# The seam between routing and the expert tiles: ranks ahead of an up product, paddings on two queues, sums ahead of the first weights' low part

## The chip, the cores and the metric

The kernel runs on one core of a Trainium2 chip. A core has five engines, each with a queue of its own that runs in order: TensorE (PE, matmuls), VectorE (DVE), ScalarE (ACT), GpSimd (POOL) and SyncE (SP, which here issues DMAs). They meet at semaphores. The metric is the device time of one execution in microseconds, lower being better.

## What is computed

Two layers over x of shape (4, 1024, 256), each with a cross attention and a feed-forward part, both behind a layer norm and added under a tanh gate:

```python
x = x + jnp.tanh(g_xattn[0]) * _L0_xattn_ref(_layernorm(x), ctx_1024, ctx_1024, mask_BxS2_ik1)
x = x + jnp.tanh(g_ffn[0]) * _L0_ffn_ref(_layernorm(x), ...)     # mixture of experts
x = x + jnp.tanh(g_xattn[1]) * _L1_xattn_ref(_layernorm(x), ctx_1024, ctx_1024, ...)
x = x + jnp.tanh(g_ffn[1]) * _L1_ffn_ref(_layernorm(x), L1_ffn_w_gate, L1_ffn_w_up, L1_ffn_w_down)

def _moe_forward(x, ...):
    logits = (xt @ gate_w.T + gate_b).astype(jnp.float32)
    scores = jax.nn.softmax(logits, axis=-1)
    top_w, top_i = jax.lax.top_k(scores, TOPK)                   # 2 of 8 experts
    ...
    outs = jax.vmap(expert)(w1, b1, w3, b3, w2, b2)              # silu(x w1) * (x w3), then w2
    y = jnp.einsum('etd,te->td', outs, gate_dense)
    z = jax.nn.silu(xt @ ws1.T + bs1) * (xt @ ws3.T + bs3) @ ws2.T + bs2   # shared expert
    return (y + z).reshape(Bq, Sq, D)
```

## The kernel before

The order on every engine is written out by hand; waits on named semaphores tie the engines together. The program has three stages.

**Blocks.** The 4096 tokens are taken in eight blocks (f = 0 to 7) of 512: first attention, second layer norm, the shared expert and the routing. The last block's share of this, f = 7, stands by itself behind the loop, and this is where the change works. On PE, `up(f, m)` for m = 0 to 3 makes a gate half (first bank) and an up half (second bank) of the shared expert's hidden columns, 12 wide matmuls each; `gate_back`, `rank`, `counts`, `pair_limits`, `single_limits` and `tables` are small groups set between them. `down(7, ...)` is the shared expert's second product, with keep-warm matmuls of fixed number before and behind it (24 and 16 rows in the trace).

**Routing.** DVE finds the two best experts of each token (`route_a`), their one-hot form and its sum `routed` (`route_b`), the differences for the softmax (`route_a2`). PE's `rank` counts, by a triangular matrix, the place of each token in its expert's list. DVE's `route_d` and `route_d2` make of it `rrow`, `rank_base` and `pos`. With `pos` POOL scatters the tokens' rows to `rows_by_expert` in DRAM, eight indirect DMAs a block (L677). After the last block PE's `counts` sums up; DVE makes `padpos`, the first free row of each expert, and in three more rounds with PE the tables `tile_expert` and `tile_row`, which tell each expert tile its weights and its rows. SP writes 128 rows of zeros behind each expert's rows ("paddings", 8 DMAs of 128 KB, L475 and L476): for each it reads a register from `padpos` and issues a DMA.

**Expert tiles.** `NU` = 40 tiles, 31 of 256 rows and 9 of 128. `load_weights(u)` and `load_tile(u)` on SP read their place from the tables into a register (L498, L481) and issue the DMA (L502, L494). ACT makes the weights' high part `wph`, DVE the low part `wpl` (`weights_low`, L2384). PE transposes the rows (`tx`, L1322) and runs three matmuls for each product. The first `tx` waits for `shared_done`, which DVE's `shared_out` of the last block gives, and then reads a register.

**Last stage.** Second layer: gathers of the experts' outputs by POOL, attention, feed-forward.

For the shared expert ACT makes the silu of the gate half, DVE's `hidden(f, m)` (L2139) adds the bias and multiplies with the up half, ACT's `hidden_high` makes the high part `hh` and DVE's `hidden_low` (L2053) the low part `hl`. For f = 7, `up(7, 2)` waits for `hidden(7, 0)`, `up(7, 3)` for `hidden(7, 1)`, `down` for `hidden(7, 2)`, and its part k = 3 for `hl` of m = 3.

Of the kernel before, what the change touches and what calls it, by code (L numbers as in the profile page):

```python
# [7 lines left out]
NE, F = 8, 256  # L8
SF, LF = 512, 768
DH, NH = 16, 16  # L10
P = 128
KD = D // P
T = B * S
GT = 4
# [33 lines left out]
def flamingo_kernel(nc, i, out):  # L48
    ctx = ExitStack()
    with ctx:  # L50
        sems = {}

        def sem(name):
            if name not in sems:
                sems[name] = ctx.enter_context(nc.semaphore(name))
            return sems[name]
# [325 lines left out]
        def _(sp):  # L382
# [88 lines left out]
                    small(vo_kept, vo0.rearrange("p b d -> p (b d)"), "l1_out")  # L471

            sp.wait_ge(sem("padpos_done"), 1)
            for e in range(NE):
                row = sp.value_load(padpos[0:1, e:e + 1], min_val=0, max_val=SPARE - P)  # L475
                sp.dma_start(xs[bass.ds(row, P), :], zeros).then_inc(sem("pad_out"), 16)  # L476

# [10 lines left out]

            def load_tile(u):
                src = rows_of_unit(xs, u, 0)  # L490

                if u >= 4:
                    sp.wait_ge(sem("tx_done"), u - 3)
                sp.dma_start(tile_of(xg[u % 4], u), src).then_inc(sem(f"tile_in{u % 4}"), 16)  # L494
# [15 lines left out]
            sp.wait_ge(sem("table_done"), 1)  # L510
            load_weights(0)
            sp.wait_ge(sem("table_done"), 3)
            sp.wait_ge(sem("spare_out"), 16 * 4)
            for p in range(2):
                sp.wait_ge(sem(f"scattered{p}"), NG // 2 * 2 * GT * 16)
            sp.wait_ge(sem("pad_out"), 16 * NE)
            load_tile(0)
            load_tile(1)
            load_weights(1)
# [346 lines left out]
        def _(act):  # L866
# [58 lines left out]
            def silu(f, m):  # L925
                act.wait_ge(sem("u_done"), MS * f + m + 1)

                if above_zero(MS * f + m - 1):
                    act.wait_ge(sem("hl_done"), MS * f + m - 1)
                n = slice(0, now(f) * P)  # L930
                act.activation(sil[m % 2][:, n], up_bank(f, m)[0], ACT.Silu, bias=bs13[:, 0, m:m + 1])\
                    .then_inc(sem("silu_done"), 1)
# [129 lines left out]
            silu(f, 0)  # L1062
            hidden_high(f, 0)
            silu(f, 1)
            hidden_high(f, 1)
            silu(f, 2)
            hidden_high(f, 2)
# [249 lines left out]
        def _(pe):  # L1317
# [390 lines left out]
                last.then_inc(sem("count_mm"), 1)  # L1708

            up(f, 0, lambda: gate_back(f))  # L1710
            up(f, 1, lambda: rank(f))
            counts()
            up(f, 2, pair_limits)
            single_limits()
# [291 lines left out]
        def _(dve):  # L2006
# [163 lines left out]
            def route_b(f):  # L2170

                dve.wait_ge(sem("topi_done"), GT * (f + 1))
                for k in range(2):
                    tt(onehot[:, k, :, :], expert_no.unsqueeze(1).broadcast_to([P, GT, NE]),
                       top8i[:, :, k:k + 1].broadcast_to([P, GT, NE]), ALU.is_equal).then_inc(sem("onehot_done"), 1)
                dve.wait_ge(sem("topi_done"), GT * (f + 1))
                cp(expert_all[:, bass.ds(f, 1), :, :].rearrange("p a k j -> p (a k) j"),
                   top8i[:, :, 0:2].rearrange("p j k -> p k j")).then_inc(sem("route_kept"), 1)
                dve.wait_ge(sem("onehot_done"), 2 * (f + 1))
                tt(routed, onehot[:, 0, :, :], onehot[:, 1, :, :], ALU.add).then_inc(sem("routed_done"), 1)  # L2180

            def route_c(f):

# [147 lines left out]
                step(g, g % 2, nxt=(g + 1 < NG), more=(g + 2 < NG))  # L2331
            f = NG - 1
            route_a(f)
            route_a2(f)
            route_b(f)
            route_d(f)
            route_d2(f, 1, NG // 2 - 1)

# [43 lines left out]
            def weights_low(u):  # L2382
                dve.wait_ge(sem("high_done0"), EARLY[0] + u + 1)
                tt(wpl[u % 2], wraw[u % 3], wph[u % 2], ALU.subtract).then_inc(sem("low_done0"), 1)  # L2384

            hidden(f, 0)
            tile_counts()
            tile_shift()
            hidden_low(f, 0)
# [9 lines left out]
            hidden_low(f, 3)  # L2399
            shift_kept()  # L2400
            route_c(f)
            weights_low(0)
            shared_out(f, 1, (0,))
            shared_out(f, 1, (1,))

            def rows_low(u):
# [431 lines left out]
```

## Time and profile before

| | us |
|---|---|
| timed executions, three | 584.28, 588.28, 591.34 |
| their median | 588.28 |
| the profiled execution | 584.31 |
| span of its instructions | 582.5 |
| PE busy | 561.4 (96%) |
| DVE busy | 452.8 (78%) |
| ACT busy | 376.4 (65%) |
| POOL busy | 258.6 (44%) |

### The profile page before, as it was taken

The page shows a single profiled execution, that of the slowest core. Times are in us where ns is not written, and L with a number is a line of the kernel's source. Part 1 is how long each engine was busy: PE and PEld are TensorE (multiplying, and loading weights), DVE is VectorE, ACT ScalarE, POOL GpSimd, SP SyncE. Part 2 cuts the span into 40 slices and gives each one's busy share as a digit, 9 for nine tenths or more (in the row PEclk, how much of TensorE's full clock was granted, in tenths as well). Part 3 has the DMA queues.
Part 4 walks back from the last instruction along what each step waited for, and adds up shares of the span by engine and source line. Part 5 has one row for each costly group of instructions (what it writes and reads, how often), then busy time and mean ns, then how long its engine had stood idle before and what let it go on. Part 6 is the DMA issues. An engine that isn't in the chain of part 4 may idle for free.

```text
span 582.5 us, 12974 instructions
## 1 busy us (share of the span) xinstructions
PE 561.4 (96%) x3950; PEld 463.8 (80%) x3950; DVE 452.8 (78%) x1248; ACT 376.4 (65%) x729; POOL 258.6 (44%) x291
## 2 busy tenths in 40 slices
PE   8999999999989999999999999989999999999997
PEld 7788888987758999999999998876746656665664
DVE  6989887977636787778887884586999899978765
ACT  5778667776514877768777773255585685785733
POOL 3456557555550134545543444668663740510100
PEclk9999899999979999999999999999999999999999
DMA  8334554352237878888998854762122241100000
GB/s 236 124 121 158 200 191 167 137 186 96 103 134 221 314 238 263 268 271 246 287 279 264 262 191 163 273 231 72 59 64 75 74 151 56 57 17 37 38 37 36
DMA packets 48117, 93.15 MB, mean 160 GB/s; under 512 B 7006, under 2 KB 17322, under 8 KB 47922
## 3 DMA queue, kind: packets, MB, share of 16 engines
q1 hardware_dynamic: 39884, 74.34, 37.8%
q0 software_dynamic: 7440, 17.97, 10.3%
q8 instruction: 33, 0.54, 0.4%
q14 instruction: 34, 0.28, 0.2%
q10 hardware_dynamic: 726, 0.02, 0.1%
HBM read 61.32 MB, written 32.17 MB: 160 GB/s over the span
## 4 chain that ended last, share of the span: by engine, by line
PE 65%; DVE 13%; issue 6%; ACT 5%; POOL 4%; SPq 3%; another core or an unknown queue 2%; DMA 2%; ACTq 0%; DVEq 0%; POOLq 0%
PE bank L1387 13%; PE bank L1389 12%; PE bank L1388 12%; PE bank L1908 10%; PE bank L1322 4%; PE bank L1930 3%; PE bank L1932 3%; POOL yr L775 2%; PE bank L1374 2%; PE bank L1870 2%; POOL rs L789 1%; DVE st L2491 1%; DVE x L2120 1%; SPq L475 1%
## 5 line engine op out<-in xcount | busy, mean ns | idle before, releaser
L727 POOL TENSOR_TENSOR yg<-yg,b 128x512 f32<-128x512 f32 x31 | 46.8, 1510 | 94.4 <-ACT yg L868 94.2
L677 POOL DMA_INDIRECT rows_by_expert<-n,pos x64 | 65.3, 1020 | 36.5 <-DVE pos L2214 20.8
L775 POOL DMA_INDIRECT yr<-expert_out,out_row x64 | 65.2, 1018 | 29.8 <-issue 19.3
L1387 PE MATMUL bank<-xTh,wph 128*128 128x256 f32 x248 | 72.3, 292 | 0.3 <-issue 0.2
L1389 PE MATMUL bank<-xTh,wpl 128*128 128x256 f32 x248 | 70.1, 283 | 0.0
L1388 PE MATMUL bank<-xTl,wph 128*128 128x256 f32 x248 | 70.1, 283 | 0.0
L1908 PE MATMUL bank<-m4Th,wint 128*128 128x512 f16 x192 | 69.0, 380 | 0.9 <-ACT m4Th L868 0.5
L1908 PE MATMUL bank<-m4Tl,wint 128*128 128x512 f16 x192 | 68.9, 379 | 0.4 <-issue 0.4
L2384 DVE TENSOR_TENSOR wpl<-wraw,wph 128x1024 fp32r<-128x1024 f32 x40 | 49.0, 1224 | 11.5 <-ACT wph L868 11.4
L868 ACT ACTIVATE wph<-wraw 128x1024 fp32r<-128x1024 f32 x40 | 42.3, 1058 | 14.3 <-PE bank L1389 9.4
L1387 PEld LDWEIGHTS bank<-xTh,wph 128*128 128x128 f32 x248 | 47.3, 191 | 0.7 <-issue 0.6
L1388 PEld LDWEIGHTS bank<-xTl,wph 128*128 128x128 f32 x248 | 47.4, 191 | 0.0
L1389 PEld LDWEIGHTS bank<-xTh,wpl 128*128 128x128 f32 x248 | 47.4, 191 | 0.0
L1136 ACT ACTIVATE n<-xa,nb,rs 128x256 f32<-128x256 f32 x64 | 34.5, 591 | 14.2 <-DVE nb L2508 13.9
L2564 DVE SCALAR_TENSOR_TENSOR sl<-bank,sl 128x512 f32<-128x512 f32 x48 | 32.7, 687 | 13.7 <-ACT sl L1183 9.9
L1930 PE MATMUL bank<-wint,g3h 128*128 128x256 f16 x192 | 42.6, 273 | 0.6 <-DVE sl L2564 0.5
L1932 PE MATMUL bank<-wint,g3l 128*128 128x256 f16 x192 | 42.5, 272 | 0.0
L868 ACT ACTIVATE g3h<-sl 128x512 f16<-128x512 f32 x48 | 30.0, 626 | 15.8 <-DVE sl L2564 15.1
L1387 PE MATMUL bank<-w2h,hTh 128*128 x142 | 40.3, 284 | 0.0
L1389 PE MATMUL bank<-w2h,hTl 128*128 x142 | 40.2, 283 | 0.0
L1388 PE MATMUL bank<-w2l,hTh 128*128 x142 | 40.2, 283 | 0.0
L1183 ACT ACTIVATE sl<-bank 128x512 f32<-128x512 f32 x48 | 28.0, 589 | 16.5 <-PE bank L1908 12.0
(359 smaller groups left out, 1727.9 us busy)
## 6 DMA issues: line engine op xcount, KB each, us to landing
wraw<-in_wexp SPq DMA_DIRECT2D x40, 512.0 KB, 4.6
xg<-rows_by_expert SPq DMA_DIRECT2D x31, 256.0 KB, 4.1
expert_out<-yg SPq DMA_DIRECT2D x31, 256.0 KB, 3.3
x_shared<-x SPq DMA_DIRECT2D x8, 512.0 KB
xa<-x_shared SPq DMA_DIRECT2D x4, 1024.0 KB, 5.2
xin<-in_x SPq DMA_DIRECT2D x7, 512.0 KB, 3.7
out<-ost SPq DMA_DIRECT2D x7, 512.0 KB, 2.8
stage<-in_wexp SPq DMA_DIRECT2D x8, 256.0 KB, 4.0
```

Source lines behind the costliest of these rows:

```text
L677: pool.indirect_dma_start(out=xs, out_offset=bass.IndirectOffsetOnAxis(ap=pos[p][:, k, j:j + 1], axis=0), in_=n2[f % 3][:, j, :], in_offse ...
L727: pool.tensor_tensor(yg[u % 3], yg[u % 3], b2[:, bass.ds(e, 1), :].broadcast_to([P, 2, D]), ALU.add)\
L775: pool.indirect_dma_start(out=yr[:, c, k, j, :], out_offset=None, in_=ys, in_offset=bass.IndirectOffsetOnAxis(ap=out_row[:, b * GB + c, k, ...
L868: return act.activation(dst, src, ACT.Copy)
L1136: act.activation(dst[:, j, :], src[:, j, :], ACT.Identity, bias=nb3[which][:, m:m + 1], scale=rs3[which][:, m:m + 1]).then_inc(sem(done), 1)
L1387: mm(o, ah, bh, start=first, stop=False)
L1388: mm(o, ah, bl, start=False, stop=False)
L1389: return mm(o, al, bh, start=False, stop=final)
L1908: last = mm(bank[:, at + w, :], wt[:, k, m * P:(m + 1) * P], part[c][:, k, :], start=(q == 0 and k == 0), stop=(q == 1 and k == KD - 1))
L1930: mm(o, g3h[:, k, t], wdv[:, k, :], start=(k == 0 and j % 2 == 0), stop=False, skip_group_check=(j % 2 == 1))
L1932: last = mm(o, g3l[:, k, t], wdv[:, k, :], start=False, stop=(k == ML - 1 and j % 2 == 0), skip_group_check=(j % 2 == 1))
L2384: tt(wpl[u % 2], wraw[u % 3], wph[u % 2], ALU.subtract).then_inc(sem("low_done0"), 1)
```

## The change

1. In the last block PE's `rank(7)` goes from the middle of `up(7, 1)` (behind the gate half) to ahead of it.
2. In `route_b`, for all blocks, `routed` is made ahead of the copy of the expert numbers. In the last block `route_b` goes ahead of `route_a2`, and DVE's `hidden(7, 0)` from behind `route_d2` to ahead of `route_d`.
3. The paddings of experts 4 to 7 are issued by ACT, between its `silu(7, 1)` and `hidden_high(7, 1)`; SP keeps those of experts 0 to 3.
4. SP reads the first tile's row number ahead of the waits for scatters, spare rows and paddings.
5. DVE's `shared_out` of the last block goes ahead of `weights_low(0)`.

```diff
             sp.wait_ge(sem("padpos_done"), 1)
-            for e in range(NE):
+            for e in range(NE // 2):
                 row = sp.value_load(padpos[0:1, e:e + 1], min_val=0, max_val=SPARE - P)
                 sp.dma_start(xs[bass.ds(row, P), :], zeros).then_inc(sem("pad_out"), 16)
...
             def load_tile(u):
                 src = rows_of_unit(xs, u, 0)
-
+                if u == 0:
+                    sp.wait_ge(sem("spare_out"), 16 * 4)
+                    for p in range(2):
+                        sp.wait_ge(sem(f"scattered{p}"), NG // 2 * 2 * GT * 16)
+                    sp.wait_ge(sem("pad_out"), 16 * NE)
...
             sp.wait_ge(sem("table_done"), 3)
-            sp.wait_ge(sem("spare_out"), 16 * 4)
-            for p in range(2):
-                sp.wait_ge(sem(f"scattered{p}"), NG // 2 * 2 * GT * 16)
-            sp.wait_ge(sem("pad_out"), 16 * NE)
             load_tile(0)
...
             silu(f, 1)
+            act.wait_ge(sem("filled"), 1)
+            act.wait_ge(sem("padpos_done"), 1)
+            for e in range(NE // 2, NE):
+                row = act.value_load(padpos[0:1, e:e + 1], min_val=0, max_val=SPARE - P)
+                act.dma_start(xs[bass.ds(row, P), :], zeros).then_inc(sem("pad_out"), 16)
             hidden_high(f, 1)
...
             up(f, 0, lambda: gate_back(f))
-            up(f, 1, lambda: rank(f))
+            rank(f)
+            up(f, 1)
             counts()
...
+                dve.wait_ge(sem("onehot_done"), 2 * (f + 1))
+                tt(routed, onehot[:, 0, :, :], onehot[:, 1, :, :], ALU.add).then_inc(sem("routed_done"), 1)
                 dve.wait_ge(sem("topi_done"), GT * (f + 1))
                 cp(expert_all[:, bass.ds(f, 1), :, :].rearrange("p a k j -> p (a k) j"),
                    top8i[:, :, 0:2].rearrange("p j k -> p k j")).then_inc(sem("route_kept"), 1)
-                dve.wait_ge(sem("onehot_done"), 2 * (f + 1))
-                tt(routed, onehot[:, 0, :, :], onehot[:, 1, :, :], ALU.add).then_inc(sem("routed_done"), 1)
...
             route_a(f)
+            route_b(f)
             route_a2(f)
-            route_b(f)
+            hidden(f, 0)
             route_d(f)
             route_d2(f, 1, NG // 2 - 1)
...
-            hidden(f, 0)
             tile_counts()
...
             route_c(f)
-            weights_low(0)
             shared_out(f, 1, (0,))
             shared_out(f, 1, (1,))
+            weights_low(0)
```

On PE, behind `up(7, 0)`, before (L1387 to L1389 are the wide matmuls of `up`, L1514 to L1518 the rank, L1682 and L1683 the counts):

```order
731 L1387 MATMUL bank<-n2Th,wsh 128x512
732 L1388 MATMUL bank<-n2Tl,wsh 128x512
733 L1389 MATMUL bank<-n2Th,wsl 128x512
734 L1514 MATMUL bank<-routed,tri 128x32
...
738 L1518 MATMUL bank<-rank_base,onesb 128x32
739 L1387 MATMUL bank<-n2Th,wsh 128x512
```

and changed (L1392 to L1394 and L1519 to L1523 are the same operations):

```order
725 L1392 MATMUL bank<-n2Th,wsh 128x512
726 L1393 MATMUL bank<-n2Tl,wsh 128x512
727 L1394 MATMUL bank<-n2Th,wsl 128x512
728 L1519 MATMUL bank<-routed,tri 128x32
...
732 L1523 MATMUL bank<-rank_base,onesb 128x32
733 L1392 MATMUL bank<-n2Th,wsh 128x512
```

The rank stands six wide matmuls earlier; twelve wide ones instead of six lie between it and the counts.

On DVE, in the last block's routing, before (`sil` is what `hidden` writes):

```order
359 L2167 TENSOR_TENSOR dlog<-logit,top_151 128x4x8
360 L2168 TENSOR_TENSOR dlog<-top_151 128x4
361 L2174 TENSOR_TENSOR onehot<-expert_no,top8i 128x32 x2
362 L2177 CAST expert_all<-top8i 128x8
363 L2180 TENSOR_TENSOR routed<-onehot 128x32
364 L2199 TENSOR_TENSOR rrow<-bank,expert_row 128x32
...
370 L2139 SCALAR_TENSOR_TENSOR sil_131<-bank,bs_58,sil_131 128x512
371 L2341 TENSOR_TENSOR padpos<-bank,expert_row 1x8
```

and changed:

```order
359 L2180 TENSOR_TENSOR onehot<-expert_no,top8i 128x32 x2
360 L2183 TENSOR_TENSOR routed<-onehot 128x32
361 L2185 CAST expert_all<-top8i 128x8
362 L2173 TENSOR_TENSOR dlog<-logit,top_151 128x4x8
363 L2174 TENSOR_TENSOR dlog<-top_151 128x4
364 L2145 SCALAR_TENSOR_TENSOR sil_131<-bank,bs_58,sil_131 128x512
365 L2205 TENSOR_TENSOR rrow<-bank,expert_row 128x32
...
371 L2348 TENSOR_TENSOR padpos<-bank,expert_row 1x8
```

`routed` stands three operations earlier, and `hidden(7, 0)` ahead of `rrow` instead of behind it.

On ACT, in the last block, changed; before, row 190 stood straight behind row 173:

```order
173 L931 ACTIVATE sil_132<-bank,bs_58 128x512
174 L1068 TENSOR_LOAD padpos
175 L1068 ISA x2
176 L1069 ISA
177 L1069 DMA rows_by_expert<-zeros 128x256
...
190 L868 ACTIVATE hh<-sil_132 128x512
```

Four such register reads with their DMAs now stand between the second silu and the high part.

## Rows read from the trace of the kernel before

**Rows 1.** Stage windows: stretch, busy PE PEld DVE ACT POOL, clock, DMA, GB/s.

```profile
161.00:165.00 4.00, 1.68 (x8) 1.23 (x8) 2.81 (x15) 1.21 (x2) 1.59 (x2) 1.00 0.18 66
165.00:172.00 7.00, 7.00 (x25) 4.47 (x24) 2.16 (x12) 1.32 (x2) 5.17 (x7) 0.52 0.48 169
172.00:184.00 12.00, 11.96 (x105) 11.37 (x105) 6.24 (x16) 4.31 (x6) 0.92 (x1) 1.00 0.54 175
200.00:360.00 160.00, 160.00 (x1300) 156.54 (x1299) 127.67 (x190) 115.81 (x217) 72.79 (x66) 1.00 0.78 245
```

**Rows 2.** Timeline of PE: start, length, operation, idle before it with its releaser.

```profile
157.72 0.40 PE L1389 MATMUL bank<-n2Th,wsl 128*128 128x512 f32 x1
...
159.47 0.18 PE L1518 MATMUL bank<-rank_base,onesb 128*128 128x32 bf16 x1
...
162.71 0.17 PE L1682 MATMUL bank<-onesb,rank_base 128*8 128x1 bf16 x1 [1.57 <-DVE rank_base L2208]
...
163.74 0.50 PE L1387 MATMUL bank<-n2Th,wsh 128*128 128x512 f32 x1 [0.76 <-DVE sil L2139]
...
166.68 0.63 PE L1388 MATMUL bank<-n2Tl,wsh 128*128 128x512 f32 x1
167.10 0.63 PE L1389 MATMUL bank<-n2Th,wsl 128*128 128x512 f32 x1
...
176.63 0.38 PE L1476 MATMUL bank<-bs,ones 128*128 128x512 bf16 x1
...
182.99 1.95 PE L1334 MATMUL bank<-ident 128*128 128x128 f32 x16
185.84 0.87 PE L1322 MATMUL bank<-identr,xg 128*128 128x128 f32 x8 [0.90 <-DVE x L2148]
```

**Rows 3.** Timeline of DVE.

```profile
158.33 0.19 DVE L2180 TENSOR_TENSOR routed<-onehot 128x32 bf16<-128x32 f32 x1
162.05 0.19 DVE L2199 TENSOR_TENSOR rrow<-bank,expert_row 128x32 f32<-128x32 f32 x1 [3.53 <-remote]
...
162.49 0.16 DVE L2208 TENSOR_TENSOR rank_base<-rank_base,rsum 128x8 bf16<-128x8 bf16 x1
...
174.62 0.19 DVE L2377 TENSOR_SCALAR tile_expert<-bank 1x40 int32<-1x40 f32 x1 [3.90 <-remote]
...
175.54 0.73 DVE L2139 SCALAR_TENSOR_TENSOR sil<-bank,bs,sil 128x512 f32<-128x512 f32 x1
...
179.62 0.69 DVE L2053 TENSOR_TENSOR hl<-sil,hh 128x512 fp32r<-128x512 f32 x1 [1.29 <-ACT hh L868]
...
183.52 1.40 DVE L2148 SCALAR_TENSOR_TENSOR x<-bank,gains,x 128x512 f32<-128x512 f32 x2
```

**Rows 4.** Timeline of ACT.

```profile
158.16 0.69 ACT L931 ACTIVATE sil<-bank,bs 128x512 f32<-128x512 f32 x1 [1.40 <-issue]
...
176.31 0.63 ACT L868 ACTIVATE hh<-sil 128x512 fp32r<-128x512 f32 x1 [6.58 <-DVE sil L2139]
...
181.28 1.06 ACT L868 ACTIVATE wph<-wraw 128x1024 fp32r<-128x1024 f32 x1 [1.70 <-DMA wraw<-in_wexp]
```

**Rows 5.** Timeline of SP's DMA issues.

```profile
164.81 12.30 SPq L476 DMA_DIRECT2D rows_by_expert<-zeros  x8
177.96 0.43 SPq L502 DMA_DIRECT2D wraw<-in_wexp  x1
179.30 1.46 SPq L494 DMA_DIRECT2D xg<-rows_by_expert  x2
```

**Rows 6.** Timeline of POOL: the last of eight scatters, with the gap before each.

```profile
171.96 0.96 POOL L677 DMA_INDIRECT rows_by_expert<-n,pos  x1 [0.30 <-issue]
```

**Rows 7.** Chain of waits, in order of time: the second, fourth and fifth padding on SP.

```profile
165.96 0.34 SPq L476
...
170.15 0.70 SPq L476
...
173.01 0.69 SPq L476
```

## The prediction

> **What bounds the kernel now.** I read the stage windows first [rows 1]. In the expert stage (200 to 360 us) TensorE (PE) is busy 160.00 of 160.00 us at the full clock, so that stage can only begin earlier, not run shorter. Ahead of it, at the seam between the last routing block (f = 7) and the first expert tile, PE does not run freely: from 161 to 165 us it is busy 1.68 of 4.00 us, and from 165 to 172 us it is "busy" throughout but at a granted clock of 0.52. The seam is what the change edits. I then followed PE through it [rows 2]. It stands 1.57 us ahead of the counts (L1682) for `rank_base`, 0.76 us ahead of the third up product for DVE's `hidden(7, 0)`, runs matmuls of 0.63 us instead of 0.40 us, and waits 0.90 us ahead of the first tile's transposes (L1322 at 185.84). DVE [rows 3] shows why: `routed` ends at 158.52, the rank matmuls end at 159.65 [rows 2], yet `rrow` starts only at 162.05, 2.40 us behind the matmul that it waits for (releaser "remote": the profile doesn't name it). All DVE work of the counts, `hidden(7, 0)` and `padpos` stands behind that wait. SP [rows 5] then issues eight paddings in 12.30 us, from 164.81, and the first weights only at 177.96, the first tile at 179.30.
>
> **The rank group and PE.** Now PE does the second half of up(7, 0) (its last matmul starts at 157.72, the next could at about 157.95, [rows 2]), then the first six matmuls of up(7, 1), and only then the rank. In the changed kernel the rank comes straight behind up(7, 0). It then has to wait for `routed`. DVE gets there sooner, since three small operations that stood ahead of it (two `dlog`, the copy of the expert numbers) move behind it; an operation like `routed` takes 0.19 us [rows 3], partly beside the next one, so that the three are worth 0.2 to 0.3 us: it comes near 158.3 instead of 158.52. Cost: PE idles about 0.3 us (157.95 to 158.3). Rank ends near 158.6, and all twelve matmuls of up(7, 1) follow, to about 161.4. Their pitch at the full clock is 0.24 us: six of them stand between the rank's last one (159.47) and the idle that ends at 162.71 after 1.57 us, so 159.50 to 161.14 with the tail of the last. Before, up(7, 1) ended at 161.14.
>
> `hidden(7, 0)` now stands ahead of `rrow` on DVE. Its input, the first silu, ends at 158.85 [rows 4], so it ends at about 159.6 and no longer makes PE wait. The price is that `rrow` cannot start before 159.6. How late the rank's signal is, I bound from both sides: 0 (the other end) and 2.40 us (this trace), so `rrow` at 159.6 to 161.0 instead of 162.05. `rank_base` follows 0.60 us behind `rrow` (162.05 to 162.65, [rows 3]): 160.2 to 161.6. PE is done with up(7, 1) at 161.4, so even the late end costs only 0.2 us. Counts, then the third up product at about 161.5 to 161.8 instead of 163.74. **Gain on PE: 2.1 us.**
>
> **The clock.** Both idle pieces of PE, 1.57 and 0.76 us, fall within the thin stretch ahead of the drop at 165; in their place stand about 0.3 and at most 0.3 us. If the clock then stays at its upper level (2.4 GHz), the twelve wide matmuls that ran at the lower one (1.2 GHz), at a pitch of 0.42 us (166.68 to 167.10, [rows 2]), go at 0.24: 12 x 0.18 = 2.2 us; the small matmuls between them fill the rest of the 7.0 us and bring some 0.7 more, so 2.9 us. The lower bound is 0 (it falls anyway), the upper 7.0 x 0.48 = 3.4 us [rows 1]. I take 2.9, since the stretches in which PE was kept busy (172 to 184 us in [rows 1]) kept the full clock. **Sum on PE: 2.1 + 2.9 = 5.0 us**, so `down(7)` starts near 171.6 instead of 176.63, and the end of the second keep-warm (182.99 + 1.95, [rows 2]) comes at 179.9 instead of 184.94. The two keep-warms themselves have fixed lengths and stay.
>
> **What must keep up for that.** (1) The sums of the last block: `shared_out` ends at 184.92 now, since the 1.23 us subtraction of the first weights stood ahead of it [rows 3]; PE's keep-warm ended at 184.94, so moving it is worth nothing by itself (0.02 us). In the new place it is what keeps 5.0 from becoming 3.8 if the weights' high part is late: the sums end 0.75 us behind `down(7)`, at 178.8, and the low part follows to 180.0, hidden behind the transposes of the first tile. The 0.90 us of PE before these (a register read behind the waits) stays: first transposes at 180.8 instead of 185.84.
> (2) ACT. It gets four paddings ahead of `hh(1)`. No row shows one on ACT; the nearest are SP's: 1.15 us from one to the next where they are dense (164.81 to 165.96), 2.86 us where they are sparse (170.15 to 173.01) [rows 5, 7]. In the mean 12.30 + about 1 us over eight is 1.67 us. Nothing excludes less than 1.15, but it would gain nothing, as follows. They start at about 162.2 (behind the second silu) and end at 166.8, 168.9 or 173.6 us. From there `hh`, silu and `hidden(7, 2)` take 0.63 + 0.69 + 0.73 = 2.0 us [rows 3, 4], and from the end of `hidden(7, 2)` to the end of `hl(3)` it is 4.03 us (175.54 + 0.73 to 179.62 + 0.69, [rows 3]), a chain that ran 3.7 us behind the start of `down(7)` at 176.63. So `down(7)` can start at 171.6 if the paddings end by 169.3. Dense ones leave 2.5 us, mean ones 0.4 us. I take the dense price, because SP's first three, issued while the same scatters ran, had it. DVE also stood 3.90 us for `tile_expert`, again with releaser "remote" [rows 3]; if its signal is as late as the rank's was, up to 2.4 us, `hidden(7, 2)` ends at 171.4 to 171.7 and costs 0 to 0.1 us.
> (3) SP. Four paddings instead of eight; before, from about 163.8 to 177.1. `padpos` now comes near 161.9 to 163.0, SP is free at about 167 to 169 and then waits for the table (168 to 170, as PE reaches that point 5 to 7 us sooner). First weights 169 to 171 instead of 177.96, landed 3.3 us later (ACT took them at 181.28, [rows 4, 5]): hidden. The tile's row number is read before the waits, about 0.7 us off the way from the last scatter to the load. The scatters themselves start when `pos` is ready, 160.9 to 162.0 instead of 163.10, and end at 170.8 to 172.0 instead of 172.92 [rows 6]; the last lands 1 to 2 us later. First tile issued at 173.0 to 174.5 instead of 179.30, needed at 180.8. The second weights (third in SP's queue) go at 175.5 to 177 instead of 181.54, as far ahead as before.
> (4) In blocks 0 to 6 `routed` comes ahead of one copy, some 0.08 us sooner; the rank there stands behind half a `down`, so this is 0.
>
> A rule of the Trainium skill weighs against the split. [Rows 5] show 12.30 us of issue for eight transfers of 128 KB. The page "DMA: Bandwidth & Descriptors", section "Issuing engines are not separate DMA queues", says that starting transfers from several engines saves only the sequencer's time, usually small beside the transfer. By that the split would be worth nothing and the loads would lead anyway. By the rows the issue is the long part; with eight paddings left on SP the second weights would go near 180 and hold PE for 1 to 2 us of the 5.
>
> **The forecast** is 5.0 us less. Made on the profiled execution (584.31 us, span 582.5) that is 579.3. That execution lies at the low end of the three timed ones (584.28 to 591.34, median 588.28), so I put the same step on their median: 583.3 us, a ratio of 0.991.
>
> **Rivals.**
> - The clock falls anyway. The rank's wait leaves a hole of its own and the counts are still thin work, and nothing in [rows 1] says how much idling was needed. Then only 2.1 to 2.6 us come: 585.9.
> - ACT pays the high price, 2.86 us a padding. Paddings end at 173.6, `down(7)` starts at 175.9: gain 0.7 us, 587.6.
> - Slower: the six sequencer steps of a padding (as the trace has them on SP) each take on ACT the 0.70 us that an SP instruction took in the sparse stretch [rows 7]. That is 4.2 us a padding, 16.8 in all, ending at 179.0; `hidden(7, 2)` at 181.0, `down(7)` at 181.3 instead of 176.63, so 4.6 us slower: 592.9. It decides from 3.1 us a padding on. Against it: even SP's sparse ones took 2.86.
> - The early start is not kept: weights or tiles late in the first expert tiles, or the gain lost in later waits. Gain 0 to 3 us: 587.
>
> **Chances.** Forecast 0.54; clock anyway 0.20; dear paddings 0.12; given back 0.08; slower 0.06. The forecast's own spread is 4 to 5.6 us, and the medians compared here wander by some us, since the three runs lie 4.0 below and 3.1 above theirs. Low end: 588.3 - 5.6 less that wandering, 577.5. High end: takes in the clock, the dear paddings and part of the case given back, with the same wandering above no change, 589.5; the slower rival stays outside. A measurement of this kernel can tell about 1% (5.9 us) from no change. The forecast is 0.85%, so nearly half of its chance may read as over 1%: faster 0.26. Slower by over 1% needs that rival with some wandering: 0.06. Same 0.68.
>
> **What would show it.** Right: no drop of the granted clock between 161 and 180 us; `hidden(7, 0)` ahead of `rrow` at about 159; L1682's twin starting without idle at 161.4; four paddings on ACT in 4 to 5 us ahead of `hh(1)`; the first expert transposes at 180 to 181.5. Wrong: a clock of 0.5 at 162 to 170; ACT's paddings lasting beyond 169.3 and PE idle in `down(7)`; PE idle ahead of the first or second tile with a DMA as releaser; or the whole shift there, but gone by 360 us.

## The result, and the profile after

The changed kernel takes 594.12 us in the median of four executions (592.21 to 597.52), the kernel before 587.27 us (584.28 to 591.34): a ratio of 1.0111, 95% interval 1.0066 to 1.0156. It is slower, by some 6.9 us, where 5.0 us less was forecast. (The ratios here and below leave out executions in a second, slower state of a chip and are not the quotients of the medians beside them; the two differ by up to 0.5%.) The profiled execution took 595.71 us, with a span of 593.9 us.

Stage windows of the changed kernel, in the columns of [rows 1]:

```profile
165.00:172.00 7.00, 2.08 (x10) 1.15 (x8) 0.00 (x0) 0.00 (x0) 5.48 (x6) 0.99 0.31 112
172.00:184.00 12.00, 6.10 (x37) 4.38 (x37) 3.33 (x18) 1.89 (x3) 2.01 (x3) 0.58 0.34 120
```

From 165 to 172 us DVE and ACT do nothing at all and PE is busy for only 2.08 us; POOL alone works throughout. Then the clock falls: 0.58 in the mean of 172 to 184. PE's timeline, in order of time (`gate_back` L1510, rank, counts, pair limits, second keep-warm, first expert transposes):

```profile
159.75 0.42 PE L1510 MATMUL bank<-ident,logitT 16*128 16x16 f32 x4
...
162.30 0.18 PE L1523 MATMUL bank<-rank_base,onesb 128*128 128x32 bf16 x1
...
165.30 0.17 PE L1687 MATMUL bank<-onesb,rank_base 128*8 128x1 bf16 x1
165.40 0.18 PE L1688 MATMUL bank<-rank_base,onesb 128*128 128x8 bf16 x1
...
166.68 0.40 PE L1394 MATMUL bank<-n2Th,wsl 128*128 128x512 f32 x1
177.90 0.59 PE L1693 MATMUL bank<-excl,cnt_f 8*128 8x8 f32 x2 [10.81 <-DVE cnt_f L2352]
...
194.15 1.95 PE L1339 MATMUL bank<-ident 128*128 128x128 f32 x16
196.01 0.87 PE L1327 MATMUL bank<-identr,xg 128*128 128x128 f32 x8
```

The counts are done at 165.58 with no idle ahead of them, as forecast (the 1.57 us of [rows 2] are gone). Then PE stands 10.81 us. DVE and ACT show for whom:

```profile
162.53 0.75 DVE L2145 SCALAR_TENSOR_TENSOR sil<-bank,bs,sil 128x512 f32<-128x512 f32 x1
163.71 0.19 DVE L2205 TENSOR_TENSOR rrow<-bank,expert_row 128x32 f32<-128x32 f32 x1 [0.43 <-PE bank L1523]
...
177.19 0.15 DVE L2348 TENSOR_TENSOR padpos<-bank,expert_row 1x8 int32<-1x8 f32 x1 [12.51 <-remote]
```

```profile
176.48 0.69 ACT L931 ACTIVATE sil<-bank,bs 128x512 f32<-128x512 f32 x1 [12.53 <-remote]
178.32 3.61 ACTq L1069 DMA_DIRECT2D rows_by_expert<-zeros  x4
```

`padpos` needs only the counts, which PE had done at 165.58, and starts 11.61 us behind them. ACT's second silu needs only up(7, 1), whose last matmul starts at 164.97, and starts at 176.48. Two engines that wait for nothing but PE are held alike: it is PE's signals that are late, not one engine's work. SP, which waits for `padpos`, follows ([rows 5] began at 164.81):

```profile
178.41 3.65 SPq L476 DMA_DIRECT2D rows_by_expert<-zeros  x4
185.03 0.43 SPq L506 DMA_DIRECT2D wraw<-in_wexp  x1
186.36 1.45 SPq L498 DMA_DIRECT2D xg<-rows_by_expert  x2
```

What else went on then is on POOL, at the border between the scatters of block 6 and of block 7:

```profile
162.27 0.96 POOL L677 DMA_INDIRECT rows_by_expert<-n,pos  x1 [0.30 <-issue]
163.54 0.96 POOL L677 DMA_INDIRECT rows_by_expert<-n,pos  x1 [0.31 <-issue]
164.80 0.96 POOL L677 DMA_INDIRECT rows_by_expert<-n,pos  x1 [0.30 <-DVE pos L2220]
...
173.65 0.96 POOL L677 DMA_INDIRECT rows_by_expert<-n,pos  x1 [0.30 <-issue]
```

`pos` is ready by the end of block 6's last scatter, so sixteen scatters follow each other with about 0.30 us between them, from 154.14 to 174.61. Scatters that follow each other like this, without a pause, are called a row below. Before, the trace has a pause of over 2 us ahead of the last eight, which began at 163.10.

**Where the time is.** I measure the seam from `gate_back` to the first expert transposes, since neither end is touched: 156.10 to 185.84 = 29.74 us before, 159.75 to 196.01 = 36.26 us after, so 6.5 us more. Of the 11.4 us between the spans, 3.65 had gone before `gate_back` and 1.2 came behind the first transposes. Part of the 3.65 is a low clock early in this execution, in untouched work (0.51 in this window, where the kernel before had 1.00):

```profile
8.00:15.00 7.00, 7.00 (x40) 7.00 (x39) 3.54 (x13) 4.27 (x14) 0.79 (x2) 0.51 1.05 292
```

The seam's 6.5 is close to the 6.9 between the medians.

### The profile page after: what moved, and what is told of

It is laid out like the page before. It is cut to its first block, busy times and chain, and to the rows that moved or that the text cites. A ratio compares the mean times of both kernels' runs of the same rounds, so it can differ in the third digit from the quotient of the medians.

```text
span 593.9 us, 12977 instructions
## 1 busy us (share of the span) xinstructions
PE 563.1 (95%) x3950; PEld 466.1 (78%) x3950; DVE 453.1 (76%) x1248; ACT 377.1 (63%) x729; POOL 258.1 (43%) x291
## 4 chain that ended last, share of the span: by engine, by line
PE 63%; DVE 13%; issue 7%; ACT 6%; POOL 4%; another core or an unknown queue 3%; DMA 3%; SPq 1%; DVEq 0%; ACTq 0%; POOLq 0%
PE bank L1392 12%; PE bank L1394 11%; PE bank L1393 11%; PE bank L1914 9%; PE bank L1327 3%; PE bank L1936 3%; PE bank L1938 3%; PE bank L1876 2%; PE bank L1379 2%; PE bank L1339 1%; POOL yr L775 1%; DMA wraw<-in_wexp 1%; DVE st L2497 1%; DVE xa L2488 1%
## 5 line engine op out<-in xcount | busy, mean ns | idle before, releaser
L1392 PE MATMUL bank<-xTh,wph 128*128 128x256 f32 x248 | 72.3, 292 | 0.5 <-issue 0.4
L1394 PE MATMUL bank<-xTh,wpl 128*128 128x256 f32 x248 | 70.1, 283 | 0.0
L1392 PEld LDWEIGHTS bank<-xTh,wph 128*128 128x128 f32 x248 | 47.2, 191 | 0.9 <-issue 0.9
L1394 PEld LDWEIGHTS bank<-xTh,wpl 128*128 128x128 f32 x248 | 47.4, 191 | 0.0
L1392 PE MATMUL bank<-w2h,hTh 128*128 x142 | 40.3, 284 | 0.7 <-DVE hTl L2446 0.7
L1394 PE MATMUL bank<-w2h,hTl 128*128 x142 | 40.2, 283 | 0.0
```

The costliest lines, as they stand in the source:

```text
L1392: mm(o, ah, bh, start=first, stop=False)
L1394: return mm(o, al, bh, start=False, stop=final)
```

## The experiments

Theory A: PE's signals are held while POOL's scatters follow each other; the early rank brings `pos` so soon that POOL's pause goes. Rival B: ACT's paddings or DVE's new order bring it. Rival C: it falls out so by chance. All ratios are to the kernel before, run on the same chip in the same job: e1 to e4 on one chip, e5 to e8, e9 to e11, e12 to e15 and e16 to e18 each on another.

**Undo the rank, and do it alone.** e1 is the changed kernel with

```diff
-            rank(f)
-            up(f, 1)
+            up(f, 1, lambda: rank(f))
```

> The changed kernel with the rank group alone put back into the middle of the second up product. Theory A (POOL's scatters hold back PE's signals as long as they follow each other; the earlier rank took POOL's pause between the last two batches away, and with it the gap through which the counts' signal came): the rank's signal is late again, by 1 to 2.4 us, POOL pauses 1 to 3 us between the last two batches, the counts' signal comes within 1 us, and the time is 583 to 589 us, 6 to 10 us under the changed kernel. Theory B (the paddings on ACT or the new order on DVE bring the stall): the stall of 10.8 us of PE ahead of the pair limits stays, 592 to 597 us. Theory C (the stall strikes by chance, whatever the order): anything between, with the stall in some executions only.

e2 is the kernel before with the opposite edit and nothing else.

> The kernel before with the rank group alone put ahead of the second up product. Theory A: if the rank's signal passes before the scatters of the batch before are over, POOL goes on without a pause, and PE stands some 10 us for the counts' answer: 592 to 597 us; if it is held until that batch is over, nothing comes of it: 585 to 588 us. Theory B: no stall, 585 to 588 us.

e1: 585.34 us, ratio 0.9993 (0.9957 to 1.0030). e2: 590.67 us, ratio 1.0117 (1.0086 to 1.0149). The loss goes with this one edit: without it there is none, and it alone brings one (0.7% by the medians, 590.67 to 586.53, and 1.2% by the ratio). DVE and POOL in e1:

```profile
166.90 0.19 DVE L2204 TENSOR_TENSOR rrow<-bank,expert_row 128x32 f32<-128x32 f32 x1 [2.44 <-remote]
...
167.87 0.15 DVE L2347 TENSOR_TENSOR padpos<-bank,expert_row 1x8 int32<-1x8 f32 x1
...
179.47 0.19 DVE L2383 TENSOR_SCALAR tile_expert<-bank 1x40 int32<-1x40 f32 x1 [5.30 <-remote]
```

```profile
167.95 0.96 POOL L677 DMA_INDIRECT rows_by_expert<-n,pos  x1 [2.28 <-DVE pos L2219]
...
176.80 0.96 POOL L677 DMA_INDIRECT rows_by_expert<-n,pos  x1 [0.30 <-issue]
```

POOL pauses 2.28 us again, and `padpos` comes through in it, without a wait. The last table signal falls into the next row of scatters, and `tile_expert` starts 1.71 us behind the end of that row (177.76). In e2, with none of the other four parts:

```profile
157.54 0.19 DVE L2200 TENSOR_TENSOR rrow<-bank,expert_row 128x32 f32<-128x32 f32 x1 [0.39 <-issue]
...
169.17 0.15 DVE L2342 TENSOR_TENSOR padpos<-bank,expert_row 1x8 int32<-1x8 f32 x1 [9.10 <-remote]
```

Its scatters end at 169.57. The rank's signal is prompt (0.04 us behind its matmul, under seven scatters that followed each other), the count's is 8.6 us late.

**All eight paddings back on SP** (e3: part 3 of the change undone).

```diff
-            for e in range(NE // 2):
+            for e in range(NE):
```

with the five lines in ACT's program that issue the others taken out.

> The changed kernel with all eight paddings on SP. Theory A: the stall stays, PE idle 10 to 11 us ahead of the pair limits; the time is that of the changed kernel or up to 5 us more (four more paddings of 1.1 us on SP ahead of the first weights): 593 to 600 us. Theory B in its form that ACT's paddings bring the stall: it goes, 583 to 588 us.

590.18 us, ratio 1.0071 (1.0027 to 1.0116). `padpos` still waits 9.00 us, PE 7.09 us. Rival B falls: the stall is there without ACT's paddings, and in e2 without DVE's order too.

**Hold POOL.** e4 is the changed kernel with one wait more, ahead of the last eight scatters:

```diff
+            pool.wait_ge(sem("count_mm"), 4)
             scatter(NG - 1, 1)
```

> The changed kernel; POOL holds the last block's eight scatters until the tables' matmuls have signalled (fourth count signal), so nothing follows the batch before. Theory A: no PE signal of this stretch is late by more than 1.5 us, PE goes through the up products without a stall and with the clock up, the tables are ready near 172 us; the scatters then run from 170 to 181 and the first tile waits for them, transposes near 187 to 190: 584 to 590 us. Theory B: the stall of about 10 us ahead of the pair limits stays and the late scatters come on top: 600 us or more. Theory C: as A or as B from run to run.

584.02 us, ratio 0.9995 (0.9952 to 1.0038). Nothing on PE, DVE, ACT or SP was edited, and the stall is gone:

```profile
160.56 0.15 DVE L2349 TENSOR_TENSOR padpos<-bank,expert_row 1x8 int32<-1x8 f32 x1 [1.39 <-PE bank L1689]
...
166.17 0.19 DVE L2385 TENSOR_SCALAR tile_expert<-bank 1x40 int32<-1x40 f32 x1 [1.56 <-PE bank L1712]
...
178.27 1.41 DVE L2155 SCALAR_TENSOR_TENSOR x<-bank,gains,x 128x512 f32<-128x512 f32 x2 [5.25 <-remote]
```

The first two name PE's matmul as releaser. The scatters now run from 166.42 to 176.84, and it is the sums of `down(7)` that are held until 1.4 us behind their end; PE then waits 2.30 and 1.14 us for the first tile's rows, which are scattered late. The seam is 26.72 us.

**A pause only for the first signal** (e5: the same wait with 1 instead of 4).

> The changed kernel with one wait more: GpSimd starts the last block's eight scatters only when the first count product is done, a pause of about 1 us after pos is ready. Theory A (signals of PE are held while scatters follow each other without a pause): padpos follows the first count at once, as in the run that holds them until the fourth; the later three signals fall into the batch and come 1 to 5 us late, as in the kernel before. PE's 10.8 us ahead of the pair limits shrink to under 2.5 us, the time comes to 583 to 588 us. Rival D (it is the sum of scatters, paddings and rows in flight, not the lack of a pause, that holds them): the later signals are as late as 10 us and the time stays over 590.

589.55 us, where the kernel before took 588.59: ratio 0.9998 (0.9961 to 1.0035), by the ratios some 6 us better than the unedited change on its own chip, with one wait more on POOL. `padpos` follows the count at once, and the last table signal is held again:

```profile
169.40 0.16 DVE L2349 TENSOR_TENSOR padpos<-bank,expert_row 1x8 int32<-1x8 f32 x1
...
181.46 0.19 DVE L2385 TENSOR_SCALAR tile_expert<-bank 1x40 int32<-1x40 f32 x1 [5.32 <-remote]
```

Its scatters end at 179.71. Rival D falls: the pause alone lets the count through.

**Plain DMAs in place of the scatters** (e8, work added; the waits for the scatters also count the eight new DMAs):

```diff
+            pool.wait_ge(sem("pos_done"), NG)
+            for k in range(2):
+                for j in range(GT):
+                    pool.dma_start(elsewhere[(k * GT + j) * P:(k * GT + j + 1) * P, :], ...)
+            pool.wait_ge(sem("count_mm"), 4)
             scatter(NG - 1, 1)
```

> The changed kernel with work added: at the place of the last block's scatters GpSimd issues eight plain DMAs of the same 128 KB to a tensor of their own, and the eight scatters follow behind the fourth count product. If any DMA that GpSimd issues holds PE's signals, padpos comes late again, by as long as the plain ones are issued. If it is the indirect ones alone (their addresses are made by the engine from pos), padpos follows the first count within 1.5 us, and the time is that of the run that held the scatters, or up to 3 us more.

588.55 us, ratio 1.0014 (0.9977 to 1.0050). POOL issues the eight plain ones from 164.86 on, and the counts end under them:

```profile
164.86 4.34 POOL L714 DMA_DIRECT2D elsewhere<-n  x8 [0.96 <-DVE pos L2227]
```

```profile
165.41 0.15 DVE L2355 TENSOR_TENSOR padpos<-bank,expert_row 1x8 int32<-1x8 f32 x1 [0.65 <-PE bank L1695]
```

`padpos` starts 0.42 us behind the counts (L1695, 164.81 + 0.18). This execution was one in which signals were held, for the rank's, under block 6's scatters, came 1.89 us behind its matmul (161.71 + 0.18):

```profile
163.78 0.19 DVE L2212 TENSOR_TENSOR rrow<-bank,expert_row 128x32 f32<-128x32 f32 x1 [1.09 <-remote]
```

So here eight plain DMAs of POOL don't hold PE's signals, and the indirect ones do.

**Scatters between the signals** (e6, on the changed kernel; e7, on the kernel before):

```diff
+            for c in range(3):
+                pool.wait_ge(sem("count_mm"), c + 1)
+                scatter(NG - 1, 1, (0,), (c,))
+            pool.wait_ge(sem("count_mm"), 4)
+            scatter(NG - 1, 1, (0,), (3,))
+            scatter(NG - 1, 1, (1,))
-            scatter(NG - 1, 1)
```

> The changed kernel with the last block's scatters set between the signals that hurt: one behind each of the first, second and third count product, the other five behind the fourth. Theory A: each of the four signals comes within about 1.3 us (one scatter) of its product; the scatters end some 3 us earlier than in the run that held all eight (at most 24 us behind the block's gate_back instead of 26), so the first tile is there earlier: 580 to 584 us, 2 us under the run that held all. Rival D: one scatter in flight already holds a signal for over 2 us, the table comes as late as the scatters gain, and the time is 584 to 588.

> The kernel before with the same pacing of the last block's scatters and nothing else. Theory A: its late table signals (3.90 us ahead of tile_expert) go, worth 2 to 3 us: 583 to 585, and 1 to 3 us over the changed kernel with the same pacing, if the change's other parts are worth anything once the signals are prompt. Rival E (the change's parts are worth nothing even then, SP's eight paddings being hidden): no difference between the two paced kernels.

e6: 585.51 us, ratio 0.9959 (0.9931 to 0.9986). e7: 590.30 us, ratio 1.0015 (0.9977 to 1.0054). In e6 the clock stays at its upper level through the seam, and the first transposes come 23.72 us behind `gate_back`: 6.0 us less than before, where the prediction had 5.0. In e7 they come at 26.39, 3.4 us less than before. But the profile of e6 gives part back at once, 6 and 16 us on:

```profile
185.84 0.35 PE L1397 MATMUL bank<-xTh,wph 128*128 128x256 f32 x1 [0.65 <-DVE xTl L2421]
...
195.81 0.36 PE L1397 MATMUL bank<-xTh,wph 128*128 128x256 f32 x1 [1.56 <-DVE wpl L2396]
```

`wpl` waits for `wph`, and that 3.60 us for its weights. From the first transposes to the end of the span it is 396.7 us before (582.5 less 185.84) and 399.4 in e6, 399.8 in e7. This also says why e7's 3.4 us don't show in its ratio. Of e2 to e7 the picture in the trace came as theory A had it, but only e4's time fell within what was expected: e2 and e3 came out lower (590.67 and 590.18 us, with PE idle for 7.78 and 7.09 us instead of some 10), e5, e6 and e7 higher. e6's 585.51 us lies where rival D had it (584 to 588), but its signals from the count on are prompt. Between e7 and e6 lie the five parts of the change: they are worth 2.7 us of the seam here, where both have a late rank signal (`rrow` 1.95 us behind the matmul in e6, 2.53 in e7) and only e7's counts wait for it.

**Price the rank where nothing is held** (e10: e6 with the rank back in the middle of up(7, 1)), **and bring the weights ahead** (e9, e11: e6 and e7 with SP's second and third weights ahead of the first tile):

```diff
-            load_weights(0)
+            for u in range(3):
+                load_weights(u)
```

> The changed kernel with paced scatters, the rank back in the middle of up(7,1). It prices the rank's move where no signal of the counts is held. By the prediction's terms the early rank is worth 2.1 us on PE in the seam: the first transposes come 1.5 to 2.5 us later behind gate_back than in the paced run (23.7 us), and the ratio lies at 0.998 to 1.000 instead of 0.996. Rival: the early rank is worth nothing even then, 23.7 us and the same ratio as the paced run.

> The changed kernel with paced scatters, and on SP the second and third weights issued ahead of the first tile instead of behind the second and third. In the paced run the first tile came 6.0 us sooner behind the block's gate_back than in the kernel before, but the second weights were issued only 1.3 us ahead of the first transposes (4.3 us in the kernel before), and PE stood 0.65 and 1.56 us in the first tiles. Theory F (given back there because the weights stand behind SP's waits for the scatters): both stalls go, 2 us less than the paced run, a ratio of 0.990 to 0.994. Rival G (the transfers are short of bandwidth, and the order on SP doesn't matter): the stalls stay or move to a later tile, a ratio of 0.995 to 0.998.

> The kernel before with paced scatters and with the second and third weights ahead of the first tile on SP, none of the five parts of the change. Theory F: the 1.56 us ahead of the third tile that the paced kernel before showed go, a ratio of 0.996 to 0.999 instead of 1.0015. What the run above with the same two edits on the changed kernel has less than this is what the five parts bring once signals come at once: about 2.7 us by the first transposes of the two paced runs.

On this chip the kernel before took 575.44 us, 2% less than on the others: e10 578.81 (ratio 1.0057, 1.0026 to 1.0087), e9 578.38 (1.0044, 1.0009 to 1.0080), e11 577.72 (1.0054, 1.0025 to 1.0083). All three lose, no ratio was as expected. The seam of e10 is 23.10 us (151.10 to 174.20), not longer than e6's 23.72, nor than the 23.68 of e6's kernel in e18, where no signal is held either: the early rank is worth nothing here. In e9 no PE idle is left 16 us behind the first transposes, but the first tile's own rows are late (1.23 and 0.74 us), and the clock is at 0.50 from 181.0 to 184.4; in e11 the later idle stays (1.45 us). Theory F is half right. And one thing didn't fit theory A. In e10 the rank ends under an unbroken row of scatters, and its signal is there at once:

```profile
153.62 0.96 POOL L677 DMA_INDIRECT rows_by_expert<-n,pos  x1 [0.30 <-issue]
154.89 0.96 POOL L677 DMA_INDIRECT rows_by_expert<-n,pos  x1 [0.30 <-issue]
```

```profile
154.47 0.18 PE L1528 MATMUL bank<-rank_base,onesb 128*128 128x32 bf16 x1
```

```profile
154.69 0.19 DVE L2209 TENSOR_TENSOR rrow<-bank,expert_row 128x32 f32<-128x32 f32 x1
```

0.04 us, where e1 with the same place of the rank waited 2.44.

**Is it the kernel or the chip?** So I ran the changed kernel (e12) and the kernel before (e13) unedited on a fourth chip, with e9's kernel again (e14) and a form with one scatter let go as soon as `pos` is there (e15).

> The changed kernel, unedited, on another chip. If the hold is the kernel's own, PE again stands 7 to 11 us ahead of the pair limits, the first transposes come 33 to 37 us behind gate_back, and the ratio to the kernel before is 1.007 to 1.012. If it hangs on the chip or on how the run falls out, the signals can be prompt, the first transposes 25 to 27 us behind gate_back, and the ratio 0.990 to 1.000.

> The kernel before, unedited, for its trace on the same chip. If the hold is the kernel's own, rrow again starts 1 to 4 us behind the last rank matmul and tile_expert waits 3 to 5 us with releaser remote, and the first transposes come 29.7 us behind gate_back. If it hangs on the chip, these can be below 1 us here. The ratio is 1.000 by construction and shows what a comparison of this kernel is worth.

> The changed kernel with paced scatters and the second and third weights ahead of the first tile, on the same chip as the two unedited kernels. If signals are held on this chip, it beats the kernel before by 0.5 to 1% and the changed kernel by 1.2 to 2%. If they are prompt here, it loses to both by some 0.4%, since pacing only delays the scatters and the first tile (PE waits 2 us for xg).

> As the run before it, but one scatter goes at once when pos is ready, one behind each of the first three count products, and four behind the fourth, so that the last ends one scatter (1.27 us) sooner. If a single scatter in flight holds a signal by no more than its own length, the first tile comes about 1.2 us sooner, 0.2% less than the run before it; if one scatter is enough to hold the count's signal for over 1.3 us, the gain is lost again.

The kernel before took 584.03 us. e12: 590.12 us, ratio 1.0097 (1.0060 to 1.0134): the loss repeats, and so does its picture (`padpos` waits 9.66 us, PE 7.76, seam 33.41). Rival C falls. e14: 581.59 us, 0.9958 (0.9933 to 0.9983). e15: 583.03 us, 0.9987 (0.9961 to 1.0012). e13, the kernel before against itself, came out at 1.0034 (1.0013 to 1.0055). That interval leaves out the truth, so I read no ratio here finer than some 0.4%: the losses of about 1% stand, the 0.4% gains of e6 and e14 don't by themselves. What stands is e14 against e12, in the same job: pacing, with the weights ahead, takes the 1% loss away.

e15 shows how little it takes. POOL and DVE:

```profile
158.43 0.96 POOL L676 DMA_INDIRECT rows_by_expert<-n,pos  x1 [0.30 <-issue]
159.69 0.96 POOL L676 DMA_INDIRECT rows_by_expert<-n,pos  x1 [0.30 <-issue]
162.43 0.96 POOL L676 DMA_INDIRECT rows_by_expert<-n,pos  x1 [1.78 <-remote]
```

```profile
162.19 0.15 DVE L2352 TENSOR_TENSOR padpos<-bank,expert_row 1x8 int32<-1x8 f32 x1 [2.79 <-remote]
```

One scatter more behind block 6's row, without a pause, and the count's signal comes 1.54 us behind its end (160.65). In e14, without it, `padpos` waited 1.39 us and PE was its releaser.

e13 also corrects my reading of the kernel before. Its clock does not fall in the seam, and still the seam is 28.75 us (154.93 to 183.68), only 1.0 us shorter than in the profiled execution, since the table's signal takes what the clock gives:

```profile
172.65 0.19 DVE L2377 TENSOR_SCALAR tile_expert<-bank 1x40 int32<-1x40 f32 x1 [5.26 <-remote]
```

Its scatters end at 171.00, 1.65 us ahead of this; in [rows 6] and [rows 3] it is 172.92 and 174.62, 1.70 us.

**A second chip of that kind.** e16 is the changed kernel, e17 the kernel before, both unedited, e18 that of e6.

> The changed kernel, unedited, on one more chip. If before takes 583 to 590 us here, the count's signal is held again, padpos waits 9 to 12 us, ratio 1.007 to 1.012. If before takes some 575 us, the signals are prompt by the theory that the hold is a chip's, padpos starts within 1.5 us of the counts, the seam is 23 to 25 us and the ratio 0.995 to 1.000.

> The kernel before, unedited, on the same chip. Held: rrow 1 to 3.5 us behind the rank, tile_expert 4 to 5 us of waiting with releaser remote, seam 28.5 to 30 us. Not held: rrow within 0.1 us of the rank under the scatters, tile_expert released by PE, seam 24 to 26 us, and the execution 575 us. The ratio of this unedited kernel again shows how far a comparison can be off.

> The changed kernel with paced scatters on the same chip. Held: ratio 0.993 to 0.998. Not held: pacing only delays the scatters, ratio 1.003 to 1.006, as the three paced forms showed on the third chip.

The kernel before took 576.28 us here. e16: 573.22 us, ratio 0.9968 (0.9938 to 0.9999). e17, the kernel before against itself: 573.36 us, 0.9966 (0.9942 to 0.9990). e18: 576.05 us, 1.0023 (0.9984 to 1.0061). The changed kernel does not lose here at all, and it doesn't win either: e16's ratio is that of the unedited e17. Its trace has the same sixteen scatters without a pause, 145.66 to 166.13:

```profile
155.05 0.96 POOL L677 DMA_INDIRECT rows_by_expert<-n,pos  x1 [0.30 <-issue]
156.32 0.96 POOL L677 DMA_INDIRECT rows_by_expert<-n,pos  x1 [0.30 <-issue]
157.58 0.96 POOL L677 DMA_INDIRECT rows_by_expert<-n,pos  x1 [0.30 <-issue]
```

and under them PE's signals as if there were none (counts done at 157.10):

```profile
157.13 0.15 DVE L2348 TENSOR_TENSOR padpos<-bank,expert_row 1x8 int32<-1x8 f32 x1 [1.15 <-PE bank L1688]
...
162.97 0.19 DVE L2384 TENSOR_SCALAR tile_expert<-bank 1x40 int32<-1x40 f32 x1 [1.56 <-PE bank L1711]
```

The seam is 23.67 us in e16 (151.27 to 174.94) and 24.93 in e17 (152.05 to 176.98), against 36.26 and 29.74 on the chip of the prediction. Both keep the clock. The 1.3 us between them lie ahead of the first transposes, where e17's PE waits and e16's doesn't:

```profile
173.60 1.95 PE L1334 MATMUL bank<-ident 128*128 128x128 f32 x16
176.98 0.87 PE L1322 MATMUL bank<-identr,xg 128*128 128x128 f32 x8 [1.44 <-DVE x L2148]
```

So the same program has the stall on one kind of chip and not on another (each chip served one job, so something else that differs between jobs isn't excluded). Where the kernel before takes 584 to 589 us (four jobs), every trace but e14's shows a signal held; where it takes 575 to 576 (two jobs, six traces), none does, and no wait between 145 and 185 us has the releaser remote. Pacing takes the stall away on the first kind; on the second it gains nothing (ratios of 1.0023 to 1.0057).

## Why the prediction was wrong

**The step that failed** is "How late the rank's signal is, I bound from both sides: 0 (the other end) and 2.40 us (this trace)", and with it "if its signal is as late as the rank's was, up to 2.4 us, `hidden(7, 2)` ends at 171.4 to 171.7". I took the lag for a property of one signal, of fixed length, and gave the count's signal none at all: "`padpos` now comes near 161.9 to 163.0". The runs show that a signal can stay held for most of a row of scatters: with the counts done at 165.58, `padpos` came at 177.19, 11.6 us late. The rows were there: [rows 3] has the lag twice, and in [rows 6] the row of scatters ends 1.7 us ahead of `tile_expert`. I wrote that the scatters "start when `pos` is ready, 160.9 to 162.0 instead of 163.10" and priced only their end, not what stands under them, nor that this closes POOL's pause. No rival had it: the slower one put the loss on ACT.

**The rank group, 2.1 us.** The rows came as described: `hidden(7, 0)` at 162.53 ahead of `rrow`, the counts without idle. But the idle that this removes, 1.57 us in [rows 2], was itself a held signal: in e17, with the rank in its old place, the counts follow without idle too. So the term exists only on chips that hold, and there the same edit brings the greater loss, unless POOL's pause is kept (e6 against e7).

**The clock, 2.9 us.** It fell, and for longer than before (0.58 in the mean of 12 us): it was still at 0.99 from 168 to 172 us and at 0.50 from 172 on, amid the 10.81 us of idling. Where PE did not stand (e6, e16) it stayed up, as forecast. But the two idle pieces, whose removal was to bring the clock back, don't make it fall by themselves: in e7, with the same order on PE, they are 1.70 and 0.76 us and the clock is 1.00 from 160 to 180. And on the path it was worth little before: e13 has the full clock and 1.0 us to show for it. Both terms of the 5.0 were covered by the held table signal.

**ACT's paddings.** The dense price was right: 3.61 us from the first of four to the end of the last, as on SP (3.65 us). There no scatters ran beside them; where some did, the four took 3.87 us (e1) and 4.04 (e5). The dear rivals fall.

**The sums ahead of the low part.** I let the 0.90 us ahead of the first transposes stay. They went: `shared_out` starts its second half at 194.35 and takes 0.75, 1.0 us ahead of the keep-warm's end, and the transposes follow without idle. In e16 against e17 this is the 1.3 us that is left of the whole change (no run undoes this part alone).

**Given back later.** This rival ("Gain 0 to 3 us") is what e6 shows: 6.0 us in the seam, 2.7 lost behind it. That this is because SP's weights stand behind its waits for the scatters is shown for one stall only, which went in e9 but not in e11.

## What to carry to other kernels

A wait whose releaser is "remote", while the work that it waits for has long been done, need not be a fixed latency: look which engine is busy just then, when that ends, and whether the edit lengthens that stretch or closes a pause in it. An edit that brings a result sooner also starts its other consumer sooner; here that consumer, the scatters, cost more than all else gained. And ask whether a loss is the kernel's or the chip's before building around it: one edit, the same trace of POOL, and 1% worse on one chip, equal on another.

## What the runs showed of the hardware

On the chips of four jobs out of six PE's semaphore increments came late while GpSimd issued indirect DMAs one behind the other (0.96 us each, 0.30 us between them): `padpos` waited 9.0 to 12.5 us in four executions. The held signal mostly came 1.2 to 1.8 us behind the end of the row (both of before, both of e1, and those shown of e4, e5, e13 and e15), 2.6 in the changed kernel, but 0.4 to 1.2 us ahead of the end in e2, e3 and e12, and in e1 and e5 `rest_to` was held 2.1 and 3.0 us and came through some 4 us ahead of it. A signal given just behind a row can be late too: in e3 the matmuls of the pair limits end at 170.31, 0.3 us behind it, and `pairs_to` starts at 172.47. A pause of 1.5 to 2.3 us let it through (e13, e5, before, e1), and eight plain DMAs of GpSimd didn't hold it (e8). Not every signal under a row is late: the rank's in e2 was there in 0.04 us, as was that for `pairs_to` in e1 (169.81 to 169.85, in the second scatter of its row). Which ones are held, and for how long, the runs don't settle. The Trainium skill, page "TensorE: Matmul & The Clock Gate", section "The cost: per-tile semaphore tail", says that each semaphore increment of PE adds about 26 ns to the tail behind its matmuls. e10's 0.04 us from the matmul to DVE is of that order, the held ones, 1 to 12 us, are not. What in the chip holds them, and what tells the two kinds of chip apart, no view shows, and it stays open.
